# A gated feed-forward kernel with exact weight splits: another maker for the first low chunk, scales three tiles ahead, and a new order in the prologue and the second batch

## The chip, the cores and the metric

One Trainium2 (trn2) chip, one core of it. The metric is the device time of one execution in microseconds (us), as the median of several runs; the profile is of one execution, taken by the hardware profiler. Engines: TensorE (PE), VectorE (DVE), ScalarE (ACT), GpSimd (POOL), and SyncE (SP), whose queue issues nearly all DMAs.

## The reference

x is [8, 512, 512] float32 and cond [8, 128]. With 2048 hidden columns:

```python
scale = cond @ norm_w.T + 1.0
h = x * (scale[:, None, :] * rsqrt(mean(x * x, -1) + 1e-6))
val, gate = split(h @ up_w.T)              # 2 x 2048 columns
h = val * gelu(gate)
h = round_and_clip(h * 127 / max|h|)       # per row, int8 range
w = ternary(down_w)                        # by mean|down_w|
y = h @ w.T (scaled back) + x
```

## The kernel before, in words

The kernel works through eight batches of 512 rows, and within each through 16 stages s, one for each tile of 128 value and 128 gate rows of up_w. TensorE multiplies in float16; each float32 operand is split into a high (its float16 rounding) and a low (the rest), and a product is high x high + high x low + low x high, over two halves of the contraction: six matmuls of 128x256. A stage combines a 2x2 block product from **seven** products p1 to p7 (a Strassen-like scheme, functions p1 to p7, lines 1010 to 1035), of seven weight combinations (A11, S1, S2, S4, A12, S3, A22) and seven of x. So a stage has 42 matmuls.

*Weights.* In batch 0, stage s also makes the weights of tile s+1. SyncE loads the tile into one of three staging buffers wst (load_w, line 327, which waits for the second mix step of the tile three before). VectorE finds a power-of-two scale per row (w_scale, line 723: a reduction over 128x1024 and three tiny operations), in stage s for tile s+2. GpSimd scales and mixes (w_mix, line 450: two scalings, four adds or subtractions; MIX = 6 steps counted by mix_steps) into one of two buffers wf. TensorE transposes the seven blocks in four chunks of 4, 4, 4 and 2 transposes (transpose_w, line 974) into three PSUM banks in turn (WB); chunk 0 waits for all six mix steps. ScalarE rounds each chunk to the high (w_high, line 560), VectorE subtracts to get the low (w_low, line 737), which frees the bank. The slots of tiles 4 to 15 go to a DRAM scratch (store_slot, line 332, 896 KB each) and are read back in each later batch through a ring of four (load_slot, line 336, which waits for p4 of the tile four before).

*Order.* Each engine's program is written out by hand, and each engine takes its instructions in that order. In stage s of batch 0 (lines 1114 to 1140) TensorE does p1, p5, chunk 0 of tile s+1, p4 of stage s-1, p6, chunk 1, p3, a transpose of x of batch 1, p2, chunk 2, p7, chunk 3. ScalarE (lines 646 to 672) takes snapshots of PSUM between the products (snap_u3 of s-1, snap_p1, snap_p5, snap_u2), the two halves of the gelu of s-1, the highs and some work ahead for batch 1 (squares, x_out, x_high in x_ahead, line 612; normalise), and in even stages the sum of absolute values of a piece of down_w (DW_SUM). VectorE (lines 917 to 939) does value(s-1), w_scale(s+2), its passes for x, the lows, hidden(s-1) and, after some stages, the running maximum (largest, over two to four tiles). GpSimd (lines 513 to 521) does gate_second(s-1), w_mix(s+2), then the rsqrt or the x mix. p4 of stage s-1 waits for snap_u3 of s-1.

*SyncE in batch 0* (lines 404 to 410), per s: the load of weight tile s+3, in odd s a piece of down_w (512 KB, once the sum of an earlier one is done), and the store of slot s, which waits for the lows of slot s.

*Prologue.* Scales of x from cond and norm_w, the squares and rsqrt of x, the first weights, the splits of x.

*Batch 1* besides its stages quantises batch 0 (q_scale, q_round, q_clip for one pair of tiles in each of the stages 2 to 9), turns the eight pieces of down_w into ternary form (down_clip on GpSimd at the stages of DW_CLIP, down_round on VectorE at DW_TERN, transpose_dw on TensorE at DW_T), and does the down product of batch 0 in four tiles (down_tile, 16 matmuls of 128x512 each, at the stages of DOWN_AFTER, here 10, 12, 13, 14), whose output VectorE writes a stage later (staged_out). SyncE's order is in its batch, line 359: pieces of down_w (load_dw waits for down_round) stand between slot loads. Batches 2 to 7 are the same without down_w.

## Time and profile before

| | |
|---|---|
| median of 3 runs | 823.17 us (820.63 to 823.93) |
| the profiled execution | 822.39 us, span 820.6 us |
| TensorE busy, mean granted clock | 770.3 us (94%), 0.989 |
| VectorE, ScalarE, GpSimd busy | 616.1, 428.6, 250.9 us |
| DMA | 130.88 MB, 159 GB/s |

The span runs from the first to the last instruction. Busy time counts executing instructions alone. A mean "granted clock" of 1.0 is TensorE at full speed. In the rows, "A <- B" in brackets tells what ended the idle time before an instruction, and L numbers are lines of the kernel.

### The profile page before, as it was taken

How to read it: one execution, taken by the hardware profiler on the slowest of the kernel's cores; microseconds unless marked ns; L12 is line 12 of the kernel's file. 1: busy time of each engine (PE TensorE's matmuls, PEld its weight loads, DVE VectorE, ACT ScalarE, POOL GpSimd, SP SyncE). 2: the span in 40 equal slices, each digit the busy share in tenths (PEclk: the TensorE clock that was granted, in tenths of full speed). 3: DMA queues.
4: the chain of work that ended last, by engine and by line, in shares of the span. 5: the costliest groups of instructions: out<-in, count | busy, mean ns of one | idle time of the engine just before them, and what ended most of it. 6: DMA issues, size and time to landing. Idle time of an engine off the chain costs nothing.

```text
span 820.6 us, 17515 instructions
## 1 busy us (share of the span) xinstructions
PE 770.3 (94%) x6385; PEld 636.2 (78%) x6385; DVE 616.1 (75%) x890; ACT 428.6 (52%) x997; POOL 250.9 (31%) x313
## 2 busy tenths in 40 slices
PE   5788887987999999999999999999999999999987
PEld 4677776875778897789878887789868987888853
DVE  5889798889854896389846895489657994589577
ACT  4677565564544664355543654355535654445523
POOL 4477777343421232112221232123211232111100
PEclk9999999999999999999999999999999999999999
DMA  4546662745455255443456154535545245505512
GB/s 142 208 133 205 192 213 119 295 156 166 177 184 184 65 197 182 136 173 134 149 179 228 53 194 142 187 114 179 170 163 179 94 175 185 186 32 195 187 52 77
DMA packets 34507, 130.88 MB, mean 159 GB/s; under 512 B 3224, under 2 KB 3744, under 8 KB 34464
## 3 DMA queue, kind: packets, MB, share of 16 engines
q1 hardware_dynamic: 34448, 130.30, 47.1%
q8 instruction: 27, 0.44, 0.2%
q14 instruction: 16, 0.13, 0.1%
q10 hardware_dynamic: 16, 0.00, 0.0%
HBM read 110.89 MB, written 19.40 MB: 159 GB/s over the span
## 4 chain that ended last, share of the span: by engine, by line
PE 73%; DVE 5%; DMA 2%; issue 1%; POOL 1%; ACT 1%; SPq 0%; DVEq 0%; POOLq 0%; ACTq 0%
PE A L1003 11%; PE A L1006 11%; PE A L1005 11%; PE Y L1055 11%; PE B L1006 8%; PE B L1003 8%; PE B L1005 8%; DMA xin<-in_x_dram 2%; DVE h L801 1%; PE X L971 1%; DMA dwb<-in_L_cond_down_w_dram 1%; PE X L1043 1%; DVE h L816 0%; DVE mpart L780 0%; DVE wst L848 0%
## 5 line engine op out<-in xcount | busy, mean ns | idle before, releaser
L1003 PE MATMUL A<-xT,wslots 128*128 (+1 forms) x1024 | 282.2, 276 | 14.8 <-ACT snapC L571 8.5
L1005 PE MATMUL A<-xT,wslots 128*128 (+1 forms) x1024 | 282.2, 276 | 0.0
L1006 PE MATMUL A<-xT,wslots 128*128 (+1 forms) x1024 | 282.1, 275 | 0.0
L475 POOL TENSOR_TENSOR snapC<-snapC 128x256 f32<-128x256 f32 x128 | 101.1, 790 | 463.5 <-ACT snapC L571 462.9
L1005 PE MATMUL B<-xT,wslots 128*128 (+1 forms) x768 | 210.2, 274 | 0.0
L1003 PE MATMUL B<-xT,wslots 128*128 (+1 forms) x768 | 210.2, 274 | 0.0
L1006 PE MATMUL B<-xT,wslots 128*128 (+1 forms) x768 | 210.2, 274 | 0.0
L767 DVE SCALAR_TENSOR_TENSOR h<-h,c_all,g 128x512 f32<-128x512 f32 (+1 forms) x128 | 108.3, 846 | 118.7 <-ACT g L594 117.9
L1003 PEld LDWEIGHTS A<-xT,wslots 128*128 128x128 f16 x1024 | 101.2, 99 | 30.9 <-ACT snapC L571 9.8
L1005 PEld LDWEIGHTS A<-xT,wslots 128*128 128x128 f16 x1024 | 101.2, 99 | 15.1
L1006 PEld LDWEIGHTS A<-xT,wslots 128*128 128x128 f16 x1024 | 101.3, 99 | 12.7
L1055 PE MATMUL Y<-dT,q 128*128 128x512 f16 x448 | 101.3, 379 | 2.1 <-DVE wst L826 2.1
L576 ACT ACTIVATE snapPU<-A 128x256 f32<-128x256 f32 x128 | 49.2, 384 | 97.4 <-PE A L1006 97.4
L571 ACT ACTIVATE snapC<-A 128x256 f32<-128x256 f32 x128 | 49.0, 383 | 95.0 <-PE A L1006 94.9
L761 DVE TENSOR_TENSOR h<-B,snapPU 128x512 f32<-128x512 f32 (+1 forms) x128 | 87.4, 683 | 1.2 <-PE B L1006 1.0
L589 ACT ACTIVATE g<-A,c_all 128x256 f32<-128x256 f32 x128 | 60.6, 473 | 46.7 <-PE A L1006 42.8
L1006 PEld LDWEIGHTS B<-xT,wslots 128*128 128x128 f16 x768 | 75.5, 98 | 9.0
L1005 PEld LDWEIGHTS B<-xT,wslots 128*128 128x128 f16 x768 | 75.5, 98 | 8.8
L1003 PEld LDWEIGHTS B<-xT,wslots 128*128 128x128 f16 x768 | 75.5, 98 | 8.4
L1055 PEld LDWEIGHTS Y<-dT,q 128*128 128x128 f16 x448 | 43.8, 98 | 49.1 <-issue 2.3
L780 DVE TENSOR_REDUCE mpart<-h 128x512 f32<-128x1536 f32 (+2 forms) x40 | 81.0, 2025 | 0.2
L801 DVE TENSOR_TENSOR h<-h,S 128x1024 f32<-128x1024 f32 x64 | 77.5, 1211 | 0.7 <-PE S L1049 0.7
(128 smaller groups left out, 920.1 us busy)
## 6 DMA issues: line engine op xcount, KB each, us to landing
wslots<-w_scratch SPq DMA_DIRECT2D x84, 896.0 KB, 4.7
w_scratch<-wslots SPq DMA_DIRECT2D x12, 896.0 KB, 4.6
wst<-in_L_cond_up_w_dram SPq DMA_DIRECT2D x16, 512.0 KB, 6.2
xin<-in_x_dram SPq DMA_DIRECT2D x8, 1024.0 KB, 7.3
dwb<-in_L_cond_down_w_dram SPq DMA_DIRECT2D x16, 512.0 KB, 4.5
wst<-in_x_dram SPq DMA_DIRECT2D x28, 256.0 KB, 5.4
out_dram<-wst SPq DMA_DIRECT2D x28, 256.0 KB, 5.2
xin<-in_x_dram SPq DMA_DIRECT2D x4, 256.0 KB, 5.1
```

The lines of the kernel that those rows point to most:

```text
L475: pool.tensor_tensor(snapC[:, s % 2, 0:H], snapC[:, s % 2, 0:H], snapC[:, s % 2, H:T], ALU.add)\
L571: act.activation(snapC[:, s % 2, 0:H], BA[s % 2][:, 0:H], ACT.Copy).then_inc(u3_snap, 1)
L576: act.activation(snapPU[:, s % 2, 0:H], BA[s % 2][:, 0:H], ACT.Copy).then_inc(p1_snap, 1)
L589: act.activation(g[:, s % 2, 0:H], BA[s % 2][:, 0:H], ACT.Gelu, scale=c_of(b, s, 1))\
L761: dve.tensor_tensor(h_tile(b, s), BB[s % 2][:, :], snapPU[:, s % 2, :], ALU.add).then_inc(val_ready, 1)
L767: dve.scalar_tensor_tensor(out=h_tile(b, s), in0=h_tile(b, s), scalar=c_of(b, s, 0), in1=g[:, s % 2, :], op0=ALU.mult, op1=ALU.mult).then_ ...
L780: dve.tensor_reduce(into[:, :], h_tiles(b, first, n).rearrange("p n t -> p t n"), AX.X, ALU.max, apply_absolute_value=True).then_inc(max_r ...
L801: dve.tensor_tensor(pair, pair, S[:, :].unsqueeze(1).to_broadcast([P, 2, T]), ALU.mult)\
L1003: pe.matmul(into, high, xh, start=(start and kp == 0), stop=False, skip_group_check=not start)
L1005: pe.matmul(into, high, xl, start=False, stop=False, skip_group_check=not start)
L1006: mm = pe.matmul(into, low, xh, start=False, stop=last, skip_group_check=not start)
L1055: mm = pe.matmul(bank[:, :], of[:, s * T + t * P:s * T + (t + 1) * P], dT[:, s, :], start=(s == first), stop=(s == last))
```

## The change

Batch 0: VectorE makes each tile's scale one stage earlier (w_scale(s+3)). TensorE starts chunk 0 after the third mix step. The low of chunk 0 is no longer VectorE's: TensorE adds minus the high to the transposed values in their PSUM bank (subtract_high, one matmul with a negative float16 identity), and ScalarE copies the result out as float16 (w_low_first). VectorE's small products c_first are done in seven instructions instead of 16. The stages of the x passes for batch 1 have tables of their own (..._AT_0), and GpSimd does x mix and rsqrt ahead of w_mix. Prologue: x is loaded ahead of the weights, norm_w through ScalarE's queue; rsqrt ahead of the first mix; two of the four normalising passes go to ScalarE; x is transposed ahead of the weights; highs and lows in another order. Batch 1: pieces of down_w are clipped at stages 0, 1, 2, 4, 5, 7, 8, 9 (rounded one later, transposed two later) instead of 0 to 7, the down tiles come at stages 12 to 15, and slot 15 is loaded ahead of the first output's store. The diff, cut (indentation reduced):

```diff
...
+C_AT = {1: (3, 2), 3: (5, 2), 5: (7, 2), 7: (9, 2), 9: (11, 2), 12: (13, 3)}
...
+SQUARES_AT_0 = {1: (0, 1), 2: (2, 3)}
+RMS_AT_0, REFINE_AT_0, NORMALISE_AT_0 = 3, 4, 4
+XT_AT_0 = {5: 0, 6: 1, 7: 2, 11: 3}
+XF_AT_0 = {5: 0, 6: 1, 10: 2, 11: 3}
+XMIX_AT_0 = {7: 0, 12: 1}
+XHI_AT_0 = {8: 0, 9: 1, 13: 2, 14: 3}
+XLO_AT_0 = {8: 0, 9: 1, 13: 2, 14: 3}
...
-DW_CLIP = {i: i for i in range(PIECES)}
-DW_TERN = {1 + i: i for i in range(PIECES)}
-DW_T = {2 + i: i for i in range(PIECES)}
+DW_CLIP = {s: i for i, s in enumerate((0, 1, 2, 4, 5, 7, 8, 9))}
+DW_TERN = {s + 1: i for s, i in DW_CLIP.items()}
+DW_T = {s + 2: i for s, i in DW_CLIP.items()}
+DOWN_AFTER_1 = {12: 0, 13: 1, 14: 2, 15: 3}
...
+    minus16 = sb("minus16", [P, P], F16)
...
     def store_slot(s):
-        sp.wait_ge(wlo_ready, NC * (s + 1))
+        sp.wait_ge(wlo0_ready, s + 1)
+        sp.wait_ge(wlo_ready, (NC - 1) * (s + 1))
         sp.dma_start(scratch[s - KEPT], wslots[:, slot_of(s), :]).then_inc(w_stored[(s - KEPT) % RING], 16)
...
+        if first:
+            load_slot(b, 15)
         store_y(b - 1, 0)
         load_xres(b - 1, 2)
-        load_slot(b, 15)
+        if not first:
+            load_slot(b, 15)
...
-    sp.dma_start(nw, norm_w.rearrange("(k p) c -> p k c", p=P)).then_inc(norm_w_loaded, 16)
-    load_w(0)
     for t in range(TT):
         sp.dma_start(xin[:, t, :], x_tile(x_v, 0, t)).then_inc(x0_loaded[t], 16)
-    for p in range(1, WSTAGE):
+    for p in range(WSTAGE):
         load_w(p)
...
+    pool.tensor_scalar(minus16[:, :], ident[:, :], -1.0, 1.0, ALU.mult, ALU.mult).then_inc(consts_ready, 1)
     pool.tensor_copy(ident16[:, :], ident[:, :]).then_inc(consts_ready, 1)
...
+    rsqrt(0)
     w_mix(0)
-    rsqrt(0)
     w_mix(1)
     for s in range(FT):
         if s > 0:
             gate_second(0, s - 1)
+        if s == RMS_AT_0:
+            rsqrt(1)
+        if s in XMIX_AT_0:
+            x_mix(1, XMIX_AT_0[s])
         if s + 2 < FT:
             w_mix(s + 2)
-        if s == RMS_AT:
-            rsqrt(1)
-        if s in XMIX_AT:
-            x_mix(1, XMIX_AT[s])
...
+    act.dma_start(nw, norm_w.rearrange("(k p) c -> p k c", p=P)).then_inc(norm_w_loaded, 16)
...
+    def w_low_first(p):
+        blk, n = W_CHUNKS[0]
+        act.wait_ge(wlo_psum, p + 1)
+        act.activation(w_part(p, 1, blk, n), WB[NC * p % 3][:, 0:n * KP * P], ACT.Copy).then_inc(wlo0_ready, 1)
...
     squares(0)
-    for c in range(3):
-        w_high(0, c)
+    act.wait_ge(rstd_ready, 1)
+    for t in range(2, TT):
+        act.activation(xin[:, t, :], xin[:, t, :], ACT.Copy, scale=rstd[:, t:t + 1]).then_inc(xn0_ready, 1)
     act.wait_ge(scl_ready, 1)
     for j in range(KT):
         x_out(0, j, X0[j])
-    for cut in range(2):
-        for kp in range(KP):
-            x_high(0, kp, cut)
+    x_high(0, 0, 0)
+    w_high(0, 0)
+    x_high(0, 1, 0)
+    w_low_first(0)
+    w_high(0, 1)
+    x_high(0, 0, 1)
+    x_high(0, 1, 1)
+    w_high(0, 2)
     w_high(0, 3)
...
         if s + 1 < FT:
             w_high(s + 1, 0)
         if s > 0:
-            act.wait_ge(c_ready, s)
+            act.wait_ge(c_ready, C_OP_OF[s - 1])
             gelu_first(0, s - 1)
         snap_u2(0, s)
         if s + 1 < FT:
+            w_low_first(s + 1)
             w_high(s + 1, 1)
         if s > 0:
             gelu_second(0, s - 1)
         if s + 1 < FT:
             w_high(s + 1, 2)
-        if s == NORMALISE_AT:
+        if s == NORMALISE_AT_0:
             normalise(1)
-        x_ahead(1, s)
+        x_ahead(1, s, SQUARES_AT_0, XF_AT_0, XHI_AT_0)
...
-        for t in range(TT):
+        for t in range(2 if is_first(b) else TT):
...
+    def c_first(p, n):
+        dve.tensor_tensor(c_all[:, VC * p:VC * (p + n)].rearrange("p (n v) -> p n v", v=VC)[:, :, 0:VG],
+                          c_w[:, VG * p:VG * (p + n)].rearrange("p (n v) -> p n v", v=VG),
+                          c_b[:, 0:1].unsqueeze(2).to_broadcast([P, n, VG]), ALU.mult).then_inc(c_ready, 1)
...
-            if not final and s - 1 in DOWN_AFTER:
-                staged_out(b - 1, DOWN_AFTER[s - 1])
+            down_after = DOWN_AFTER_1 if first else DOWN_AFTER
+            if not final and s - 1 in down_after:
+                staged_out(b - 1, down_after[s - 1])
...
-    w_scale(0)
...
+    refine(0)
+    normalise(0)
     dve.wait_ge(bmaxT_psum, 1)
     dve.tensor_reduce(brow[:, :], BA[1][0:B, 0:P], AX.X, ALU.max).then_inc(scl_steps, 1)
-    rms(0)
+    w_scale(0)
...
-    refine(0)
-    normalise(0)
-    w_scale(1)
-    for c in range(3):
-        w_low(0, c)
-    dve.wait_ge(scl_ready, 1)
-    c_first(0)
     for kp in range(KP):
         x_mix_first(kp)
-    for cut in range(2):
-        for kp in range(KP):
-            x_low(0, kp, cut, KP * cut + kp + 1)
+    w_scale(1)
+    x_low(0, 0, 0, 1)
+    x_low(0, 1, 0, 2)
+    w_low(0, 1)
+    x_low(0, 0, 1, 3)
+    x_low(0, 1, 1, 4)
+    w_low(0, 2)
+    w_scale(2)
+    c_first(0, 3)
     w_low(0, 3)
-    w_scale(2)
     for s in range(FT):
         if s > 0:
             value(0, s - 1)
-            if s + 2 < FT:
-                w_scale(s + 2)
-        if s == RMS_AT:
+        if s + 3 < FT:
+            w_scale(s + 3)
+        if s == RMS_AT_0:
             rms(1)
-        if s == REFINE_AT:
+        if s == REFINE_AT_0:
             refine(1)
-        if s in XLO_AT:
-            x_low(1, *divmod(XLO_AT[s], 2), XLO_AT[s] + 1)
+        if s - 1 in XLO_AT_0:
+            x_low(1, *divmod(XLO_AT_0[s - 1], 2), XLO_AT_0[s - 1] + 1)
         if s == FT - 2:
             c_later()
+        if s in C_AT:
+            c_first(*C_AT[s])
         if s + 1 < FT:
-            w_low(s + 1, 0)
-            c_first(s + 1)
             w_low(s + 1, 1)
         if s > 0:
             hidden(0, s - 1)
@@ -940,6 +976,7 @@
...
+    staged_out(0, TT - 1)
...
@@ -964,24 +1001,46 @@
...
-            pe.wait_ge(xn_ready, TT * b + TT)
+            pe.wait_ge(xn_ready, TT * b + 2)
+            if is_first(b):
+                pe.wait_ge(xn0_ready, 2)
...
+    def low_done(at):
+        p, c = divmod(at, NC)
+        if c == 0:
+            pe.wait_ge(wlo0_ready, p + 1)
+        else:
+            pe.wait_ge(wlo_ready, (NC - 1) * p + c)
+    def subtract_high(p):
+        blk, n = W_CHUNKS[0]
+        pe.wait_ge(whi_ready, NC * p + 1)
+        pe.matmul(WB[NC * p % 3][:, 0:n * KP * P], minus16[:, :], w_part(p, 0, blk, n), start=False, stop=True,
+                  skip_group_check=True).then_inc(wlo_psum, 1)
...
         if c == 0:
+            pe.wait_ge(mix_steps, MIX * p + 3)
+        elif c == 1:
             pe.wait_ge(mix_steps, MIX * (p + 1))
         if at >= 3:
-            pe.wait_ge(wlo_ready, at - 2)
+            low_done(at - 3)
         for a in range(n):
             for kp in range(KP):
-                tr = pe.transpose(WB[at % 3][:, (a * KP + kp) * P:(a * KP + kp + 1) * P],
-                                  wf(p)[:, blk + a, kp * P:(kp + 1) * P], ident[:, :])
+                tr = pe.matmul(WB[at % 3][:, (a * KP + kp) * P:(a * KP + kp + 1) * P],
+                               wf(p)[:, blk + a, kp * P:(kp + 1) * P], ident[:, :], is_transpose=True,
+                               start=(a == 0 and kp == 0), stop=(a == n - 1 and kp == KP - 1),
+                               skip_group_check=True)
...
-            pe.wait_ge(wlo_ready, NC * s + CHUNK_OF[a] + 1)
+            low_done(NC * s + CHUNK_OF[a])
...
-            if not final and s in DOWN_AFTER:
-                if first and s == min(DOWN_AFTER):
+            down_after = DOWN_AFTER_1 if first else DOWN_AFTER
+            if not final and s in down_after:
+                if first and down_after[s] == 0:
                     pe.wait_ge(dT_ready, PIECES)
-                down_tile(b - 1, DOWN_AFTER[s])
-
-    pe.wait_ge(consts_ready, 1)
+                down_tile(b - 1, down_after[s])
+    pe.wait_ge(consts_ready, 2)
...
-    for c in range(3):
-        transpose_w(0, c)
     for j in range(KT):
         transpose_x(0, j, X0[j])
+    transpose_w(0, 0)
+    transpose_w(0, 1)
+    subtract_high(0)
+    transpose_w(0, 2)
     transpose_w(0, 3)
...
         p6(0, s)
         if s + 1 < FT:
+            subtract_high(s + 1)
             transpose_w(s + 1, 1)
...
```

## Rows read from the trace of the kernel before

**Rows 1.** The page, busy time, share of the span, instructions.
```profile
PE 770.3 (94%) x6385; PEld 636.2 (78%) x6385; DVE 616.1 (75%) x890; ACT 428.6 (52%) x997; POOL 250.9 (31%) x313
```

**Rows 2.** Windows: busy us of each engine by stretch, clock, DMA.
```profile
core 0: us, PE busy (x) PEld busy (x) DVE busy (x) ACT busy (x) POOL busy (x), PEclk, DMA share, GB/s
...
34.20:148.00 113.80, 96.16 (x813) 83.99 (x811) 95.33 (x171) 76.92 (x178) 80.17 (x102) 0.96 0.51 168
...
152.00:260.00 108.00, 98.04 (x831) 80.11 (x829) 79.85 (x104) 54.21 (x121) 40.36 (x42) 0.97 0.55 191
260.00:350.00 90.00, 89.96 (x762) 74.57 (x760) 66.07 (x91) 46.18 (x112) 20.52 (x26) 1.00 0.47 158
```

**Rows 3.** Timeline, ScalarE: first snapshot of stages 1 and 15 of batch 0.
```profile
35.46 0.39 ACT L576 ACTIVATE snapPU<-A 128x256 f32<-128x256 f32 x1
...
148.16 0.39 ACT L576 ACTIVATE snapPU<-A 128x256 f32<-128x256 f32 x1
```

**Rows 4.** Timeline, TensorE: fourth weight chunk in stages 0 and 1.
```profile
33.86 0.38 PE L983 MATMUL Y<-ident,q 128*128 128x128 f32 x2
...
39.97 0.38 PE L983 MATMUL Y<-ident,q 128*128 128x128 f32 x2
```

**Rows 5.** Waits in 34 to 148 us: us in total, times, longest.
```profile
POOL q L456 <- DVE inv_w L735: 21.8, 13, 4.4
...
PE Y L983 <- POOL q L468: 6.1, 5, 2.1
...
PE S L983 <- POOL q L468: 5.9, 4, 2.4
PE A L1003 <- ACT snapC L571: 5.2, 3, 3.7
...
PE S L983 <- DVE wslots L741: 0.4, 1, 0.4
```

**Rows 6.** Groups by shape in 34 to 148 us: busy us, mean ns.
```profile
L741 DVE TENSOR_TENSOR wslots<-Y,wslots 128x512 f16<-128x512 f32 x28 | 19.1, 683 | 5.2 <-ACT wslots L567 5.0
L567 ACT ACTIVATE wslots<-Y 128x512 f16<-128x512 f32 x28 | 16.8, 599 | 14.0 <-PE Y L983 13.5
...
L462 POOL TENSOR_TENSOR q<-q 128x256 f32<-128x256 f32 x13 | 11.4, 877 | 0.0
...
L468 POOL TENSOR_TENSOR q<-q 128x256 f32<-128x256 f32 x14 | 10.2, 726 | 1.1
...
L669 ACT ACTIVATE dwb<-dwb 128x1024 f32<-128x1024 f32 x8 | 8.4, 1049 | 0.0
```

**Rows 7.** Timeline, stage 12 of batch 0.
```profile
131.52 0.84 ACT L557 ACTIVATE xT<-xf 128x768 f16<-128x768 f32 x1 [4.18 <-POOL xf L483]
...
134.00 0.40 PE L1003 MATMUL A<-xT,wslots 128*128 128x256 f16 x1 [3.66 <-ACT snapC L571]
```

**Rows 8.** Timeline, prologue.
```profile
6.67 0.63 ACT L540 ACTIVATE xf<-xin 128x512 f16<-128x512 f32 x1 [4.00 <-DMA xin<-in_x_dram]
...
12.09 1.03 POOL L448 TENSOR_TENSOR r_pow<-ms,neg_half 128x4 f32<-128x4 f32 x1
...
26.05 0.39 PE L1003 MATMUL A<-xT,wslots 128*128 128x256 f16 x1 [6.27 <-DVE xT L720]
```

**Rows 9.** The tile wst up to 150 us: the landing of its loads.
```profile
DMA to landing us min/median/max: 3.3/6.2/8.8
```

**Rows 10.** Batch 1: waits in 152 to 260 us, SyncE's slot 10, landing.
```profile
PE Y L991 <- DVE wst L848: 6.1, 2, 3.2
...
PE A L1003 <- ACT snapC L571: 3.4, 2, 2.3
...
ACT xT L557 <- POOL xf L483: 1.5, 1, 1.5
...
202.03 0.43 SPq L339 DMA_DIRECT2D wslots<-w_scratch  x1
...
wslots<-w_scratch SPq DMA_DIRECT2D x84, 896.0 KB, 4.7
```

More of the change, by code:

```diff
@@ L61, in gated_ffn_program @@
     B12 = T1
+    C_AT = {1: (3, 2), 3: (5, 2), 5: (7, 2), 7: (9, 2), 9: (11, 2), 12: (13, 3)}
+    C_OPS = 1 + len(C_AT)
+    C_OP_OF = [1 if p < 3 else 1 + next(i + 1 for i, (q, n) in enumerate(C_AT.values()) if p < q + n) for p in range(FT)]
     W_CHUNKS = [(0, 2), (2, 2), (4, 2), (6, 1)]
@@ L262, in gated_ffn_program @@
         rstd_ready = sem("rstd_ready")
+        xn0_ready = sem("xn0_ready")
         xn_ready = sem("xn_ready")
@@ L274, in gated_ffn_program @@
         whi_ready = sem("whi_ready")
+        wlo_psum = sem("wlo_psum")
+        wlo0_ready = sem("wlo0_ready")
         wlo_ready = sem("wlo_ready")
@@ L610, in normalise, with x_ahead @@
                     act.activation(xin[:, t, :], xin[:, t, :], ACT.Copy, scale=rstd[:, t:t + 1]).then_inc(xn_ready, 1)
-            def x_ahead(b, s):
-                if s in SQUARES_AT:
-                    squares(b, SQUARES_AT[s])
-                if s in XF_AT:
-                    x_out(b, XF_AT[s])
-                if s in XHI_AT:
-                    x_high(b, *divmod(XHI_AT[s], 2))
+            def x_ahead(b, s, squares_at=SQUARES_AT, xf_at=XF_AT, xhi_at=XHI_AT):
+                if s in squares_at:
+                    squares(b, squares_at[s])
+                if s in xf_at:
+                    x_out(b, xf_at[s])
+                if s in xhi_at:
+                    x_high(b, *divmod(xhi_at[s], 2))
             def batch(b, first=False, final=False):
@@ L672, in _ @@
                     w_high(s + 1, 3)
-            act.wait_ge(c_ready, FT + VC)
+            act.wait_ge(c_ready, C_OPS + VC)
             batch(1, first=True)
@@ L742, in w_low @@
                     .then_inc(wlo_ready, 1)
-            def c_first(p):
-                pair = slice(VG * p, VG * p + VG)
-                dve.tensor_scalar(c_all[:, VC * p:VC * p + VG], c_w[:, pair], c_b[:, 0:1], None, ALU.mult)\
-                   .then_inc(c_ready, 1)
+            def c_first(p, n):
+                dve.tensor_tensor(c_all[:, VC * p:VC * (p + n)].rearrange("p (n v) -> p n v", v=VC)[:, :, 0:VG],
+                                  c_w[:, VG * p:VG * (p + n)].rearrange("p (n v) -> p n v", v=VG),
+                                  c_b[:, 0:1].unsqueeze(2).to_broadcast([P, n, VG]), ALU.mult).then_inc(c_ready, 1)
             def c_later():
@@ L882, in _ @@
             dve.tensor_copy(cndT, BA[0][:, 0:B]).then_inc(condT_ready, 1)
-            w_scale(0)
+            rms(0)
             dve.wait_ge(scl_psum, 1)
@@ L1130, in _ @@
                 if s + 1 < FT:
+                    subtract_high(s + 1)
                     transpose_w(s + 1, 1)
                 p3(0, s)
-                if s in XT_AT:
-                    transpose_x(1, XT_AT[s])
+                if s in XT_AT_0:
+                    transpose_x(1, XT_AT_0[s])
                 p2(0, s)
```

## The prediction, made before the changed kernel was built or run

> **What bounds the kernel now.** I read the page first: TensorE is busy most of the span and VectorE three quarters of it [rows 1]. Then the windows, by stretch, since these shares are means: batches 2 and later are full, TensorE being busy 89.96 of 90 us there, and nothing in the diff touches their work. What can move is the prologue, batch 0 (113.8 us with TensorE busy 96.2, clock 0.96) and batch 1 (108.0 us with 98.0 busy) [rows 2]. The stage starts give batch 0 its pace: from the second stage's snap at 35.46 to the last one's at 148.16 are 14 stages in 112.7 us, 8.05 us each [rows 3]. The least that TensorE needs is in its fastest stage, from one fourth weight chunk to the next: 39.97 - 33.86 = 6.11 us [rows 4]. So 14 x 6.11 = 85.5, and 4 x 0.44 for the 16 transposes of x that fall into this stretch (0.109 each, as 56 instructions take 6.11): 87.3. The trace shows the stage in full there: 42 products and 14 transposes. **25.4 us are excess.** The chain of waits tells whose: TensorE waits 6.1 + 5.9 = 12.0 us for GpSimd's last mix of a tile, 5.2 for ScalarE's snapshot, 0.4 for a low; GpSimd before it waits 21.8 us in 13 mixes for the scales of VectorE [rows 5]. So the circle is value, scale, mix (two scalings and four adds of 0.73 to 0.88 us, some 4.9 [rows 6]), transpose. The other 7.8 us are hand-offs and the low clock: a mean of 0.96 over 113.8 us is 4.6 us, and the granted clock falls to 1.2 from 2.4 GHz behind long waits; after the wait of 3.66 us a product matmul shows 400 ns where the fastest stage starts an instruction every 0.109 us [rows 4, 7].
>
> **Batch 0, part by part.** *Scales three ahead, mix released after its third step.* The scales of tile s+2 are now written a stage before the mix needs them, so the 21.8 us of GpSimd's wait go. GpSimd's own work is 80.2 us of this stretch, 5.7 per stage [rows 2], and its in-order queue keeps the snapshot sum ahead of the mix, so it still can be late at the two stages with x mixes of some 3.4 us (four adds): I leave 1.0 of the 12.0 us. Gain 11.0.
> *Low of chunk 0 by TensorE and ScalarE.* VectorE loses one pass of 0.683 us per tile, and nine of sixteen tiny products [rows 6]: some 0.8 us of 6.8 per stage (95.3 / 14 [rows 2]). It is not the last releaser in rows 5 except for 0.4 us, so I price the relief at 0.4. TensorE gains one matmul of 512 columns per tile: two 256-column slots of 0.109 us 0.22 x 14 = 3.1 us, all on the path. ScalarE gains a pass of 0.60 us (as its highs of the same shape [rows 6]) per tile: from 76.9 us to 85.3, 6.1 per stage [rows 2], as much as TensorE's 6.3. It stands between the second snapshot and the remaining highs, so highs 1 to 3 and the snapshot that TensorE's fourth product waits for queue behind it. In stages with a down_w sum (1.05 us and its readout [rows 6]), the normalising or an x pass there is no slack. Bounds for what this adds: 0, if it fits into ScalarE's idle time (36.9 us of the stretch, 113.8 - 76.9), and 8.4, if each pass lies on the path; I take 2.5, nearer to nothing since three quarters of those 36.9 us would have to be in the wrong place otherwise.
> *x passes in another order.* At stage 12 ScalarE stood 4.18 us for GpSimd's x mix, and TensorE 3.66 behind it [rows 7]. Mix before w_mix and its high a stage later: that 3.7 goes. rsqrt(1) now stands before a mix, but its input comes some 2 us into the stage, and the mix has a stage of room: nothing, else 1 us.
> *The staging load.* The scale of tile s+3 reads a buffer whose load the SP queue issues only after the store of a slot (896 KB) and in every second stage a down_w piece. These loads land in 3.3 to 8.8 us [rows 9]; by the order of the code the issue is one stage minus 0.2 us ahead of the use where it used to be two. At 7.2 us per stage the slow ones come 1.8 us late, five times; VectorE has about 2.5 us before TensorE feels it, except after the wide maxima. I put 2.0 us on it (0 to 9).
> *Clock and hand-offs.* With the long waits gone, 4.6 us of low clock should shrink to some 1.2: gain 3.4.
> Sum: -11.0 - 0.4 + 3.1 + 2.5 - 3.7 + 2.0 - 3.4 = **-10.9 us**, 7.3 per stage.
> GpSimd's adds take 877 ns on average where the least disturbed ones take 726 [rows 6]. If any VectorE work caused that, less VectorE work would give back about 1 us more over batch 0; I take nothing.
> The Trainium skill (SBUF — State Buffer, section "SBUF: two separate sides") says that the port pair which the two share is an exclusive lock, taken by VectorE only in two-port modes or with two SBUF inputs. By that rule the dropped pass, which reads PSUM, frees nothing, and the sum would stay; no row here separates the two.
>
> **Prologue.** TensorE's first product starts at 26.05. The rsqrt starts at 12.09 though four squares from 6.67 at some 0.67 each are done at 9.4, as GpSimd was in the first mix; the first square waited 4.00 us for its x tile [rows 8]. With x tiles ahead of the weights and rsqrt ahead of the mix, the normalised x is some 4 us earlier. Of that 1.8 us (the scale of tile 0, a pass over 1024 columns and three tiny ones, which VectorE now does before the scales of x that ScalarE's x_out needs) is given back. I take **-2.2 us**; bounds 0 (the second weight scale, 1.8, now ahead of the x lows, is given back too) and -4.
>
> **Batch 1.** Its excess over a full batch is 18 us [rows 2]; the 64 transposes of down_w are in it (at most 7.0, at 0.109) and stay. The 2.3 us wait at stage 3 behind x of the next batch stays, since four slot loads and x are issued as before [rows 10]. Of the 6.1 us in which TensorE waits for the rounding of pieces (stages 6, 7), VectorE's round and one contended pass leave stage 4: -1.3. These two stages still have a round each. The wait of ScalarE for GpSimd at stage 8, 1.5 us, goes, as GpSimd doesn't hang on the last piece's load before it: -1.5. But the SP queue loads piece 7 when the sixth round is done, now at the end of stage 8, and *slot 10 is queued behind it*. Slot loads (896 KB) land in 4.7 us, and with 512 KB ahead in some 6.5 (an estimate: 512/896 of the two thirds of 4.7 that go by size). The round ends some 0.8 us into stage 9, a stage of about 4.6 + 0.4 us, so the slot lands some 2.8 us after TensorE wants it for stage 10, with 0.5 for the issue. Before it went out at 202.03, stages ahead [rows 10]. Bounds 0 (if the round runs early) and 4. Of the down tiles one leaves stage 10 and one enters 15, the same 16 matmuls on TensorE in whichever stage; VectorE's output pass of the last tile falls into the start of batch 2, where ScalarE's gelu ends last: nothing, and one pass of some 0.7 us if that cover is gone. Sum -1.3 - 1.5 + 2.8 = **0**, from -4 to +3.
>
> Total -10.9 - 2.2 + 0 = -13.1. The profiled execution took 822.39 us around its span of 820.6: 809.3. It lies 0.8 below the median of the three runs, so against that, **810 us**. A measurement of this kernel can tell about 0.5% (4.1 us) from no change.
>
> **Rivals.**
> *TensorE becomes the bound.* For it: every other engine has less than 6.3 us of work per stage. Against it: 6.1, 5.9 and 5.7 leave little for in-order queues. Batch 0 is then 87.3 + 3.1 + 1 = 91.4 for 112.7, -21.3; with the prologue -23.5: 799.7. Chance 0.17.
> *The staging load paces batch 0.* The wait for w_loaded takes the place of that for the scales: from VectorE's last low of a stage 8.8 us to the load's landing, then 6.2 us of that later stage, is 15.0 for two stages, 7.5 each, over stages 4 to 12, with the ScalarE terms on top: batch 0 gains some 7, slot 10 costs 4: 815 to 818. Chance 0.14.
> *It doesn't do what it says.* GpSimd, already 5.7 us per stage and without its wait, still delivers mixes as late since the snapshot sum holds it; then only the prologue and stage 12 are left: 819 to 822. Against it: GpSimd's wait in front of the mix is for scales, thirteen times [rows 5]. Chance 0.06.
> *Slower: the ScalarE circle.* High 0, subtract, low 0 are three dependent steps on two in-order queues. If ScalarE's queue ends each stage, already at 8.05 us, 0.60 + 0.22 us add to each: 14 x 0.82 = 11.5, less 2.2: 832. It decides from the point at which ScalarE's idle time ahead of the highs is used up in every stage; 36.9 us of it, 2.6 a stage, speak against it. Chance 0.05.
> *The forecast* itself, with its own range of 803 to 815, has 0.58.
>
> **Numbers.** Faster by over 0.5%: 0.58 + 0.17 + 0.12 of the load case: 0.87. Within 0.5%: 0.02 of that case and the 0.06: 0.08. Slower: 0.05. The range takes in the edge of the TensorE case and the load case: 801 to 819.
>
> **What would show it.** Right: GpSimd's wait for the scales under 3 us; TensorE's on the last mix under 2; stages of batch 0 at 6.9 to 7.6; VectorE waits in front of the scale's reduction on the load; first product at 23.5 to 24.5; a wait of TensorE for a slot load at stage 10 of batch 1, and no change from batch 2 on. Wrong: waits of TensorE on ScalarE over 8 us in batch 0 (ScalarE case), stages at 6.4 (TensorE case), or a batch 1 shorter by over 4 us.

## The result, and the profile after

The changed kernel takes 817.88 us (median of 6 runs, 815.63 to 819.54), the kernel before 822.73 us in the runs beside it: ratio 0.9939, 95% interval 0.992 to 0.9958, so 5 us faster. The profiled execution took 816.54 us around a span of 814.8. I had predicted 810; the time lies in the stated range of 801 to 819, but the gain is less than half of the 13 us I summed.

The page after, span and busy time (answers to [rows 1]):

```profile
span 814.8 us, 17562 instructions
...
PE 771.6 (95%) x6401; PEld 635.3 (78%) x6401; DVE 610.5 (75%) x863; ACT 437.0 (54%) x1015; POOL 251.2 (31%) x314
```

The windows after, for stage 0, the fourteen stages 1 to 14 of batch 0, stage 15, batch 1 and the rest (answers to [rows 2]; columns as there):

```profile
22.87:33.42 10.55, 8.95 (x64) 6.87 (x65) 10.03 (x17) 5.08 (x13) 10.04 (x12) 0.86 0.22 76
33.42:138.81 105.39, 96.18 (x817) 83.92 (x815) 88.33 (x144) 81.64 (x190) 76.85 (x101) 0.97 0.54 182
138.81:143.12 4.31, 4.15 (x39) 3.72 (x39) 3.80 (x5) 2.30 (x8) 0.86 (x2) 1.00 0.74 220
143.12:254.19 111.07, 98.68 (x827) 80.21 (x826) 81.84 (x105) 53.81 (x121) 40.21 (x42) 0.95 0.53 189
254.19:814.00 559.81, 553.05 (x4615) 452.44 (x4613) 413.08 (x560) 280.60 (x666) 114.72 (x141) 1.00 0.44 150
```

The bounds are starts of ScalarE's first snapshot of a stage (the first bound is TensorE's first product). With the same bounds before, [rows 3] gave 112.7 us for stages 1 to 14, and batch 1 had 107.69. So the 5.8 us of span come from three places: **stage 1 begins 2.0 us earlier** (33.42 for 35.46), **stages 1 to 14 take 7.3 us less** (105.4), and **batch 1 takes 3.4 us more** (111.1). From batch 2 on nothing moved.

The length of each stage, as the difference of two such snapshot starts, shows where (us; stage 0 first):

```
batch 0  before   7.9  5.6  9.4  6.1  7.6  7.5  7.3  7.0 12.4  5.8 10.7  7.3 11.6  7.3  7.0  4.3
         after    9.1  6.5  7.4  5.6  9.9  7.8  7.8  7.3  7.6  6.1 10.8  6.1  6.8  8.0  7.6  4.3
batch 1  before   4.6  6.3  7.8  6.3  5.0  5.0  8.5 10.5  6.9  4.8  8.0  5.0  8.0  8.0  8.0  4.7
         after    4.6  6.6  8.3  6.2  5.0  4.6  7.4  8.6  5.0 10.0  7.1  5.5  8.0  8.0  8.0  8.1
```

Stages 8 and 12 of batch 0 lost 4.8 us each. Stage 4 grew by 2.3 and stage 10 stayed at 10.8. In batch 1 stages 6 to 8 lost 4.9 together, while stage 9 more than doubled (in stages 10 and 15 a down tile of some 3.5 us has left and come, so stage 10 is 2.5 us too long).

The waits after, from 20 to 145 us (answers to [rows 5]):

```profile
POOL snapC L496 <- ACT snapC L599: 29.2, 13, 6.8
...
PE S L1040 <- DVE wslots L776: 4.8, 3, 2.1
POOL q L477 <- DVE inv_w L770: 4.2, 1, 4.2
PE A L1062 <- ACT snapC L599: 3.7, 5, 2.1
...
DVE inv_w L761 <- DMA wst<-in_L_cond_up_w_dram: 2.3, 2, 1.9
...
PE Y L1040 <- POOL q L483: 1.3, 2, 1.1
```

GpSimd's 21.8 us of waiting for scales are gone from the stages (the 4.2 left are in the prologue); it now waits for ScalarE's snapshots instead, and TensorE hardly feels that: its 12.0 us of waits for mixes are 1.7, all but 0.2 of them in stage 0. But its wait for a low (L776) went from 0.4 to 4.8 us. Here is that wait at its longest, in the timeline of stages 9 and 10:

```profile
96.43 1.36 DVE L755 TENSOR_TENSOR xT<-xf,xT 128x768 f16<-128x768 f32 x1
97.71 0.69 DVE L780 TENSOR_TENSOR c_all<-c_w,c_b 128x4 f32<-128x4 f32 x1
98.32 0.68 DVE L776 TENSOR_TENSOR wslots<-Y,wslots 128x512 f16<-128x512 f32 x1
98.92 0.81 DVE L802 SCALAR_TENSOR_TENSOR h<-h,c_all,g 128x512 f32<-128x512 f32 x1
99.76 1.92 DVE L815 TENSOR_REDUCE mpart<-h 128x512 f32<-128x1536 f32 x1
...
101.71 1.19 DVE L819 TENSOR_TENSOR m<-m,mpart 128x512 f32<-128x512 f32 x1
...
102.83 0.68 DVE L776 TENSOR_TENSOR wslots<-S,wslots 128x512 f16<-128x512 f32 x1
...
103.65 0.63 PE L1040 MATMUL S<-ident,q 128*128 128x128 f32 x4 [2.11 <-DVE wslots L776]
```

Read it upward: TensorE wants the bank S for the next tile's transposes. The low that frees it is done at 103.5, because VectorE has an x low, a small product and a wide maximum ahead of it. The mean granted clock in 100 to 112 us is 0.86.

Stage 4, ScalarE's and TensorE's timelines:

```profile
58.85 2.54 ACT L638 ACTIVATE xin<-xin,rstd 128x512 f32<-128x512 f32 x4
61.30 1.04 ACT L704 ACTIVATE dwb<-dwb 128x1024 f32<-128x1024 f32 x1
...
62.60 0.37 ACT L599 ACTIVATE snapC<-A 128x256 f32<-128x256 f32 x1
...
63.03 0.28 PE L1062 MATMUL A<-xT,wslots 128*128 128x256 f16 x1 [2.09 <-ACT snapC L599]
```

The normalising came from stage 5 to stage 4, an even stage with a sum over down_w, and the snapshot that TensorE's product p4 needs is behind both.

Batch 1: SyncE's queue and TensorE at stage 10:

```profile
200.39 0.33 SPq L366 DMA_DIRECT2D dwb<-in_L_cond_down_w_dram  x1
...
200.76 11.47 SPq L358 DMA_DIRECT2D wslots<-w_scratch  x4
...
207.86 0.40 PE L1062 MATMUL A<-xT,wslots 128*128 128x256 f16 x1 [4.14 <-DMA wslots<-w_scratch]
```

Slot 10 goes out at 200.76 behind the last piece of down_w and is there, by the end of TensorE's wait, 7.1 us later (207.86 - 200.76). TensorE stands 4.14 us, and the window of the next 8.6 us shows a clock of 0.67, where half speed (1.2 GHz for 2.4) would be 0.5:

```profile
207.86:216.48 8.62, 8.62 (x58) 6.84 (x59) 4.83 (x6) 3.90 (x9) 1.24 (x2) 0.67 0.61 235
```

The prologue, in the timeline (answers to [rows 8]):

```profile
7.76 1.03 POOL L469 TENSOR_TENSOR r_pow<-ms,neg_half 128x4 f32<-128x4 f32 x1 [5.64 <-DVE ms L724]
...
22.87 0.40 PE L1062 MATMUL A<-xT,wslots 128*128 128x256 f16 x1 [2.32 <-DVE xT L755]
```

rsqrt starts 4.3 us and the first product 3.2 us earlier. Stage 0 is then 1.1 us longer: TensorE waits 1.12 and 0.45 us in it for GpSimd's mix, in a stretch of 10.55 us in which VectorE is busy 10.03 and GpSimd 10.04.

The 2.0 us gained at the start of stage 1 are those of one profile. Six other profiles below have the same prologue and stage 0 (e1, e2, e5, e6, e11, e12), and there stage 1 begins at 33.42 to 35.27, between 0.2 and 2.0 us ahead of the old 35.46. Much of what differs is the clock: product matmuls start every 0.213 us at first and every 0.109 us later, and the faster rhythm is there by 27.2 us in this profile, in e1 only from 31.8.

### The profile page after: what moved, and what is told of

It is laid out like the page before. It is cut to its first block, busy times and chain, and to the rows that moved or that the text cites. A ratio compares the mean times of both kernels' runs of the same rounds, so it can differ in the third digit from the quotient of the medians.

```text
span 814.8 us, 17562 instructions
## 1 busy us (share of the span) xinstructions
PE 771.6 (95%) x6401; PEld 635.3 (78%) x6401; DVE 610.5 (75%) x863; ACT 437.0 (54%) x1015; POOL 251.2 (31%) x314
## 4 chain that ended last, share of the span: by engine, by line
PE 72%; DVE 6%; DMA 3%; issue 1%; ACT 1%; SPq 0%; DVEq 0%; ACTq 0%
PE A L1062 11%; PE A L1065 11%; PE A L1064 11%; PE Y L1114 11%; PE B L1065 8%; PE B L1062 8%; PE B L1064 8%; DVE h L836 2%; DMA xin<-in_x_dram 2%; PE X L1010 1%; DMA wslots<-w_scratch 1%; DMA w_scratch<-wslots 1%; DVE h L802 1%; PE X L1102 1%; DVE h L851 0%
## 5 line engine op out<-in xcount | busy, mean ns | idle before, releaser
L802 DVE SCALAR_TENSOR_TENSOR h<-h,c_all,g 128x512 f32<-128x512 f32 (+1 forms) x128 | 106.6, 833 | 122.8 <-ACT g L622 122.1
```

What stands on the lines that cost most here:

```text
L802: dve.scalar_tensor_tensor(out=h_tile(b, s), in0=h_tile(b, s), scalar=c_of(b, s, 0), in1=g[:, s % 2, :], op0=ALU.mult, op1=ALU.mult).then_ ...
```

## The experiments

Ratios are to the kernel before in the same session, with the 95% interval. The changed kernel's is 0.9939 (0.992 to 0.9958). One interval is some 2 us to either side (3 for e5), so single edits that differ by less are told apart by their traces or not at all. A difference of a few us between the stage lengths of two profiles can also be one of TensorE's clock, and the text names it where it matters.

| run | edit to the changed kernel | median us | ratio (interval) |
|---|---|---|---|
| e1 | slot 10 ahead of the last piece | 815.36 | 0.9902 (0.9877, 0.9927) |
| e2 | batch 1 as before | 814.79 | 0.9907 (0.9882, 0.9932) |
| e3 | low of chunk 0 on VectorE | 817.66 | 0.9935 (0.9913, 0.9957) |
| e4 | scales two ahead | 817.98 | 0.9935 (0.9911, 0.9959) |
| e9 | scales two ahead, mix released at six | 829.52 | 1.0092 (1.0061, 1.0124) |
| e10 | x passes as before | 816.63 | 0.9923 (0.9901, 0.9946) |
| e5 | sum of stage 4 to stage 3 | 813.75 | 0.9892 (0.9854, 0.9931) |
| e6 | maximum after the lows | 817.82 | 0.9939 (0.9915, 0.9963) |
| e11 | e2 + e5 | 811.33 | 0.9854 (0.9831, 0.9877) |
| e12 | e11 + stage 9 relieved | 810.05 | 0.984 (0.9819, 0.9862) |
| e13 | e2 + e10 | 814.01 | 0.9887 (0.9867, 0.9907) |
| e14 | *kernel before*, mix released at three | 817.64 | 0.9931 (0.991, 0.9953) |

### Batch 1: the queue behind the last piece

e1:
```diff
                 load_slot(b, 9)
                 if first:
+                    load_slot(b, 10)
                     load_dw(7, PIECES + 7)
-                for s in range(10, 15):
+                for s in range(11 if first else 10, 15):
```


> The changed kernel with one edit in SyncE's order: slot 10 is loaded ahead of the last piece of down_w. Theory A (slot 10, queued behind that piece, is what batch 1 lost): TensorE's 4.1 us wait for a slot load at stage 10 and the half-speed matmuls behind it go, batch 1 gets 5 to 6.5 us shorter than the changed kernel's 111.1, total 811 to 813. Theory B (the link is saturated whichever transfer goes first): slot 10 or 11 is late all the same, or the last piece is late for its clip and the down tiles, and the total stays at 816 to 819.

e2:
```diff
-    DW_CLIP = {s: i for i, s in enumerate((0, 1, 2, 4, 5, 7, 8, 9))}
-    DOWN_AFTER_1 = {12: 0, 13: 1, 14: 2, 15: 3}
+    DW_CLIP = {i: i for i in range(PIECES)}
+    DOWN_AFTER_1 = DOWN_AFTER
```
(and SyncE's load of slot 15 and the last staged_out where they were)

> The changed kernel with batch 1 as before (pieces of down_w at stages 0 to 7, down tiles at 10, 12, 13, 14, SyncE's old order). Theory A: the new batch 1 costs 3.4 us net by the traces (111.1 against 107.7), so undoing it alone gives 813.5 to 815.5, and the waits at stages 6 to 8 (8 us) come back while the one for slot 10 goes. Theory B (batch 1 is only shifted by where batch 0 ends, and would be as long in either order): no change, 816.5 to 819.

e1 gave 815.36, 2.5 us better than the changed kernel and between the ranges of my two theories. The wait for the slot is gone from TensorE's list and stage 9 is 6.6 us for 10.0, but stage 10 is still 6.7, and batch 1 109.5 us long. The trace names what is late next, the rounding of the pieces, now three times:

```profile
PE Y L1051 <- DVE wst L884: 6.5, 3, 2.9
```

e2, in theory A's range, gave 814.79 with batch 1 at 108.4 us: stages 6 to 8 are long again (8.1, 10.6, 6.9 us), and 9 and 10 are as before (4.8, and 8.0 with its down tile). So the slot load was the largest loss of the new batch 1, but its gain at stages 6 to 8, 4.9 us, was also partly a move: with fewer roundings there, the ones moved to stages 9 and 10 stand in front of TensorE too.

### Batch 0: the scale and mix chain

e4:
```diff
-                if s + 3 < FT:
-                    w_scale(s + 3)
+                if s > 0 and s + 2 < FT:
+                    w_scale(s + 2)
```
(and each entry of C_AT a stage later where the scale is)

> The changed kernel with scales two tiles ahead again. Theory A (the scales were the wait that paced batch 0): GpSimd's wait for them comes back with some 20 us in all, TensorE's for the mixes with over 5, batch 0 gets 5 to 8 us longer, 823 to 826. Theory B (GpSimd's wait was only slack, and the other edits carried the gain): within 1.5 us of the changed kernel's 817.9, with TensorE's wait for mixes under 3 us since the mix is released after its third step.

e9, e4 and:
```diff
                 if c == 0:
-                    pe.wait_ge(mix_steps, MIX * p + 3)
-                elif c == 1:
                     pe.wait_ge(mix_steps, MIX * (p + 1))
```


> The changed kernel with scales two tiles ahead and the mix released after all six steps: the whole scale-mix chain as before. Theory A (the two edits stand in for each other; either of them breaks the old circle): now GpSimd's mix comes late again, TensorE waits for it with 4 to 8 us, total 822 to 825. Theory B (the chain was late only where the x passes, the order of GpSimd and the chunk-0 low made it late): within 1.5 us of the run that has the scales back alone, 817 to 819.

e14, in the kernel before:
```diff
                 if c == 0:
+                    pe.wait_ge(mix_steps, MIX * p + 3)
+                elif c == 1:
                     pe.wait_ge(mix_steps, MIX * (p + 1))
```


> The kernel before with one edit: chunk 0 waits for the third mix step instead of the sixth (chunk 1 for the sixth). Theory A (that wait alone broke the old circle, the scales three ahead being its stand-in): TensorE's 12 us of waits for mixes fall under 5, batch 0 5 to 8 us shorter, total 815 to 818. Theory B (in the old frame, with the chunk-0 low on VectorE and x passes in between, an earlier chunk 0 only moves the wait to chunk 1 or to a low): 820 to 823, and TensorE's waits for lows or ScalarE grow by what the mixes lose.

e4 was the surprise: **theory B**. GpSimd waits 13.5 us for scales again, and the time is the same (817.98), with stages 1 to 14 at 104.7 us. In e4's waits TensorE has 3.2 us on mix steps, not 12, the two largest groups of it here:

```profile
POOL q L477 <- DVE inv_w L770: 13.5, 9, 2.1
...
PE Y L1040 <- POOL q L483: 1.7, 3, 1.1
PE Y L1040 <- POOL q L489: 0.9, 1, 0.9
```

With the earlier release undone as well the time is 829.5 us, 11.6 above the changed kernel and 6.5 above the kernel before (822.99 in that session), beyond the 822 to 825 of theory A. GpSimd's wait is back at its old size and TensorE waits for the last mix step (L489):

```profile
POOL q L477 <- DVE inv_w L770: 19.9, 10, 4.2
...
PE Y L1038 <- POOL q L489: 11.0, 7, 3.3
...
PE S L1038 <- POOL q L489: 3.4, 2, 2.4
```

So the early release breaks the circle, and the scales three ahead add nothing to it. Whether the scales alone, with the release after six steps, would have broken it too, no run shows. e9 also tells what the rest of the change does without the release: against the kernel before, stage 1 begins 1.9 us later, stages 1 to 14 take 1.1 us more (113.8) and batch 1 3.6 more (111.3).

I had not let the change's early release into the sum as an edit of its own at all. And e14 asks the other way round: the old kernel with the early release alone, a change to one wait, takes 817.64 us, ratio 0.9931: **as much as the whole change gave**. Stages 1 to 14 take 108.0 us for 112.7, about half of this by a mean granted clock of 0.97 for 0.95; batch 0 and all before it are 5.6 us shorter at the start of batch 1 (146.90 for 152.48). Its waits show that the scales are nearly as late as ever, and that TensorE no longer minds:

```profile
POOL q L456 <- DVE inv_w L735: 19.0, 12, 4.4
...
PE A L1005 <- ACT snapC L571: 10.2, 5, 4.7
...
PE S L985 <- DVE wslots L741: 2.8, 3, 1.4
PE Y L985 <- DVE wslots L741: 1.3, 1, 1.3
```

What it minds is ScalarE's snapshot (10.2 us for 5.2 in [rows 5]), with stages 8 and 12, the x mixes, still at 12.3 and 11.6 us. And it waits 4.1 us for lows, for 0.4 before, though nothing in VectorE's program was changed.

### Batch 0: the low of chunk 0

e3:
```diff
-                    w_low_first(s + 1)
...
-                    subtract_high(s + 1)
...
                 if s + 1 < FT:
+                    w_low(s + 1, 0)
                     w_low(s + 1, 1)
```
(likewise in the prologue, with the old counts of wlo_ready)

> The changed kernel with the low of chunk 0 back on VectorE (no subtract on TensorE, no extra ScalarE pass); batch 0 then has scales three ahead and the new x passes alone. Theory A (ScalarE's extra pass and TensorE's subtract cost about what VectorE's relief gives): within 2 us of the changed kernel, 816 to 820. Theory B (VectorE is what ends the stages now): 5 to 8 us slower, 823 to 826. Theory C (ScalarE is, and its late snapshots): 3 to 5 us faster, 813 to 815.

817.66 us: **theory A**, the extra pass and the extra matmul cost what they give. But not because nothing happens. TensorE's window of the 14 stages is 106.2 us long, VectorE is busy 95.6 of them (88.3 in the changed kernel), and TensorE's waits for lows more than double:

```profile
PE Y L1036 <- DVE wslots L773: 6.3, 6, 1.5
PE S L1036 <- DVE wslots L773: 5.5, 3, 2.7
```

With the low on VectorE, VectorE is thus what TensorE waits for most: 11.8 us for 4.8. The change's move of the low relieves TensorE of 7 us of such waiting. No run separates what takes this back, but the traces name two parts. The 14 subtract matmuls are 3.1 us; three of them stand directly in front of a wait of TensorE (1.03, 2.11 and 1.69 us) and fill time that was idle, so some 2.4 us count. The other part is the clock, whose mean in these stages is 1.00 in e3 and 0.97 in the changed kernel (some 3.2 us):

```profile
34.96:141.20 106.24, 91.15 (x808) 80.40 (x806) 95.64 (x159) 76.68 (x175) 73.99 (x101) 1.00 0.54 180
```

e10 and e11 below have 1.00 there too, with the low as in the change. So the slow stretches are no price of the subtract, and the move may be worth some 3 us that this pair of profiles hides; the medians (817.66 and 817.88) don't show it. The first product also comes later with the low on VectorE (ScalarE's first snapshot at 26.30 for 24.37).

### Batch 0: the x passes, stage 4 and stage 10

e10:
```diff
-    SQUARES_AT_0 = {1: (0, 1), 2: (2, 3)}
-    RMS_AT_0, REFINE_AT_0, NORMALISE_AT_0 = 3, 4, 4
+    SQUARES_AT_0 = SQUARES_AT
+    RMS_AT_0, REFINE_AT_0, NORMALISE_AT_0 = 4, 5, 5
```
(the other tables alike; on GpSimd rsqrt and x mix behind w_mix)

> The changed kernel with the x passes of batch 0 at their old stages and GpSimd's rsqrt and x mix behind the weight mix. Theory A (the order of the x passes carries most of the gain of batch 0: stages 8 and 12 fell from 12.4 and 11.6 us to 7.6 and 6.8): stages 8 and 12 over 10 us again, stage 4 back from 9.9 to under 8, batch 0 5 to 7 us longer, total 822 to 825. Theory B (scales and mixes carry it): stage 12 alone comes back, 3 us or less, 819 to 821.

e5:
```diff
-    DW_SUM = {2 * i: i for i in range(PIECES)}
+    DW_SUM = {(3 if i == 2 else 2 * i): i for i in range(PIECES)}
```


> The changed kernel with one ScalarE pass moved: the sum of the third down_w piece from stage 4, where the normalising now is, to the empty stage 3. Theory A (stage 4's 9.9 us come from ScalarE's queue, with 2.5 + 1.25 us of extra passes ahead of the last high and the snapshot): TensorE's 2.1 us wait for that snapshot falls below 1 and the half-speed stretch behind it goes; stage 4 at 8 to 8.7, total 815 to 816.5. Theory B (the stage is held by the low of VectorE or by the load): under 0.7 us of change, 817.5 to 818.5.

e10 fell outside both theories: 816.63 us, if anything a little below the changed kernel. Stages 8 and 12 go to 9.4 us (for 7.6 and 6.8), not over 10, and stages 4, 13 and 14 give 3.7, 1.9 and 1.2 back (6.2, 6.1 and 6.4 for 9.9, 8.0 and 7.6); stages 1 to 14 take 102.9. The new order of the x passes cured two stages and broke three others. That the sum is 2.5 us shorter with the old order isn't shown to come from it: the mean granted clock of these stages is 1.00 in e10 for 0.97, which alone is worth more.

e5 shows what the coincidence with the sum costs: one pass and its accumulation (1.04 + 0.19 us) moved to an empty stage give 813.75 us, better than my 815. That is 4.1 us by the medians, with an interval that overlaps the changed kernel's; in the profiles, stages 1 to 14 are 2.2 us shorter (103.2). TensorE's wait there goes from 2.1 to 1.5 only, stage 4 from 9.9 to 8.8, and stage 5 from 7.8 to 6.1, since it no longer starts at half speed. I had expected the wait to fall below 1 (missed) and the slow stretch to go (it did): most of the gain is clock.

e6:
```diff
                     hidden(0, s - 1)
-                    largest(0, s - 1)
                 if s + 1 < FT:
                     w_low(s + 1, 2)
                     w_low(s + 1, 3)
+                if s > 0:
+                    largest(0, s - 1)
```


> The changed kernel with the running maximum of VectorE behind the third and fourth low of each stage in batch 0 instead of ahead of them. Theory A (stage 10's 10.8 us, and TensorE's 4.8 us of waits for lows, are the wide maximum and an x low ahead of a low that frees a bank): the waits for lows fall below 1.5 us, stage 10 to under 8.5, total 813 to 815.5. Theory B (VectorE has too much work whatever its order: the wait moves to the next value or low): total within 1 us of the changed kernel, with waits of ScalarE or TensorE on VectorE elsewhere.

**Theory B.** 817.82 us, nothing. The longest stall moved from stage 10 (9.9 us, with a wait of 1.89 left) to stage 8 (12.1 us), where the maximum over four tiles, with its second pass of 1.08 us, now stands on VectorE from 78.50 to 83.4. The value pass of the next stage comes behind it, then the scale and a small product, and the low is done at 87.4 only:

```profile
87.59 0.73 PE L1041 MATMUL S<-ident,q 128*128 128x128 f32 x4 [2.63 <-DVE wslots L776]
```

e11 and e12 put the pieces together; e12 has in addition:
```diff
-                if s - 1 in XLO_AT_0:
+                if s - 1 in XLO_AT_0 and s != 9:
...
                     w_low(s + 1, 3)
+                if s == 9:
+                    x_low(1, 0, 0, 1)
```
(and C_AT's entry at stage 9 at stage 10)

> The changed kernel with batch 1 as before and the down_w sum of stage 4 at stage 3. Theory A (the two losses are apart: 3.1 us of batch 1 and 4.1 us of stages 4 and 5): they add, 810 to 812. Theory B (part of what stage 4 gave came back in batch 1 because it began at another moment): 812.5 to 814.

> As the run before, and in stage 9 the x low (0.95 us) is behind the lows and the small product of two columns' worth (0.7 us) a stage later, so 1.6 us less of VectorE's work stand ahead of the third low of stage 9, which TensorE waited 2.1 us for at stage 10. Theory A (that queue is stage 10's 10.8 us): the wait falls under 0.7 us, no half-speed stretch follows, stage 10 at 7 to 8.5, total 2 to 4 us below the run before. Theory B (VectorE is merely late by a fixed amount): the stall moves to a later stage, as when the maximum was moved, total within 1 us of the run before.

e11: 811.33 us, 1.5% below the kernel before: the two repairs add. Its interval lies clear of the changed kernel's and of e14's, so once the two losses are repaired the rest of the change is worth something beyond the early release; which part of it, no run says. e12: 810.05, not told apart from e11. The wait at stage 10's second chunk (2.11 us in the changed kernel) is gone, but the x lows still stand ahead of a low there, and the wait comes back some 3.6 us later in the trace, as 1.42 us. Stage 10 is 9.6 us, for 10.8 in the changed kernel and 10.1 in e11:

```profile
104.87 1.55 DVE L752 TENSOR_TENSOR xT<-xf,xT 128x1024 f16<-128x1024 f32 x1
...
107.24 0.63 PE L1038 MATMUL S<-ident,q 128*128 128x128 f32 x4 [1.42 <-DVE wslots L773]
```

e13 has the edits of e2 and e10.

> The changed kernel with both batch 1 and the x passes as before; what is left of the change are scales, mix release, chunk-0 low and the prologue. Theory A (the new x order costs 1 to 2 us, the new batch 1 some 3, independent of each other): 812.5 to 814.5. Theory B (with the old x passes ending later, batch 1 of the old kind suffers): 815 to 817.

814.01 us, as theory A has it, but its profile shows batch 0 short (102.9) and batch 1 long: 111.2 us in an order that took 107.7 to 108.4 in five other profiles (before, e2, e11, e12, e14). The window shows what is longer:

```profile
142.11:253.35 111.24, 100.74 (x827) 81.48 (x826) 78.11 (x104) 54.06 (x120) 39.48 (x42) 0.94 0.54 185
```

TensorE's mean granted clock is 0.94 there for 0.97 in the other five, which is some 3.3 us of 111; its waits are no longer than in e2 (10.5 us in all, for 10.6). Whether the batch got this clock from how it was entered or by chance, one profile can't say.

## Why the prediction was right and wrong

**Right.** The bound and its circle; the disappearance of GpSimd's wait for the scales and of TensorE's for the mixes (12.0 us to 0.2 in stages 1 to 14, I had 1.0 left, 11.0 gained); no change from batch 2 on; the place and the mechanism of the slot load at stage 10 of batch 1; the gains at stages 6 to 8, -4.9 for my -2.8 (2.3 to 5.1 in the seven other profiles with this order), with 1.4 us less waiting for the rounding of pieces for my 1.3.

**Right in part by luck, the prologue:** -2.0 for -2.2. The first product came at 22.87, ahead of my 23.5 to 24.5, and stage 0, which I had not priced, gave 1.1 us of it back. In the six other profiles with the same prologue the gain is 0.2 to 2.0 us.

**Wrong, batch 0: -7.3 for -10.9.** The failing step is "It is not the last releaser in rows 5 except for 0.4 us, so I price the relief at 0.4". I read VectorE's slack off a trace in which another engine was late, and let it stand for the new one. TensorE's waiting for lows was to go from 0.4 us to nothing and went to 4.8, a miss of 4.8 us, larger than the whole miss of batch 0. e14, in which VectorE's work is untouched, shows that the rhythm does it: there the early release alone takes these waits from 0.4 to 4.1 us. e3 shows that the relief was worth more than 0.4 in waiting: without it the waits are 11.8 us. VectorE's own work (88.3 of 105.4 us) comes in lumps, maxima, x lows and products ahead of a low that frees a bank. The remaining terms: subtract 2.4 for my 3.1, since 3 of the 14 matmuls fall into waits; snapshots 3.7 us now where I had 5.2 - 3.7 + 2.5 = 4.0; low clock 0.97 of 105.4 us is 3.2 for my 1.2, with slow stretches behind the stalls of stages 4 and 10; the staging load made VectorE wait 2.3 us in two waits, and no wait of TensorE is put down to it, so my 2.0 there looks too much. With the mixes, 0.8 us better than I had them, the terms add up to a miss of 3.0 us, for 3.6 measured.

**Wrong, the attribution.** I credited the scales three ahead and the early release together with 11.0 us and the x passes with 3.7. The runs: the scales three ahead, nothing on top of the release (e4), and never run without it; release alone, 5 us and more even in the old kernel (e14); both gone, +11.6 (e9); x passes, nothing that shows (e10): what stages 8 and 12 gained was paid with stages 4, 13 and 14. Stage 4's collision was to be seen in the tables: the normalising at 4, the sums at every even stage. I wrote that there was "no slack" in such stages and priced all of them at 2.5 us; that one stage and the slow stretch behind it cost 2.2 us by e5's profile and 4.1 by its median.

**Wrong, batch 1: +3.4 for 0.** The failing step is the term "so the slot lands some 2.8 us after TensorE wants it". The wait was 4.14 us (the slot landed in 7.1 us, not 6.5, and the round ended about when I had it). That two thirds of a landing go by size, on which my 6.5 rested, no row showed. And I put no price on the clock behind it, although [rows 7] had shown one: stage 10 is 2.5 us too long beside, and the mean granted clock of the batch went from 0.97 to 0.95, some 2 of its 3.4 us. My bounds for the batch, -4 to +3, just missed.

**The rivals.** TensorE as the bound: not reached, stages 7.5 us on average. The staging load pacing batch 0: refuted, 2.3 us of waits. The ScalarE circle: refuted, snapshot waits fell from 5.2 to 3.7 us. "It doesn't do what it says": GpSimd's waiting shifted to the snapshots exactly as described, but its mixes were in time all the same.

## What to carry to other kernels

When a wait between two engines is removed, an engine whose idle time you count as slack has that slack only in the old rhythm: ask which of its instructions frees what the fast engine needs next, and what lumps stand in front of it. Before building the large reordering, try the smallest edit of the wait itself: here a semaphore count that asks for three steps instead of six gave as much as the whole change. When two edits aim at the same wait, run each of them alone. And when work is moved between hand-written tables, add up each engine's extras stage by stage, and for a DMA queue what is next behind each waiting issue; both losses here were readable that way.

## What the runs showed of the hardware that I had not expected

A stall of TensorE can cost more than its length, and the same stall doesn't always. After the wait of 4.14 us the 8.6 us that followed ran at a mean granted clock of 0.67, which at two levels of 1.2 and 2.4 GHz is about two thirds of them at half speed, some 2.8 us lost; after the 2.11 us at stage 10 of batch 0 the window of 12 us has 0.86, 1.7 us lost. But e11 has the same wait of 2.11 us at the same place, and its clock from 100 to 112 us is 1.00; e3 has one of 2.74 us (at 82.3) and 1.00 in the 12 us behind it. So part of the differences between two profiles here, up to some 3 us in stages 1 to 14 and as much in batch 1, is whether the clock fell behind a stall that both have.

The granted clock in the first microseconds has to be read with care. e11's window from 23 to 27 us gives 1.00, while its product matmuls start every 0.213 us there and every 0.109 later. I therefore compare clocks only behind stage 0.

GpSimd's instructions can take up to three times their time beside VectorE. In stage 0 after, two scalings that take 0.69 us elsewhere took this, while VectorE ran x lows with both inputs in SBUF:

```profile
21.19 2.10 POOL L477 TENSOR_SCALAR q<-wst,inv_w 128x512 f32<-128x512 f32 x1 [4.16 <-DVE inv_w L770]
...
23.27 1.76 POOL L479 TENSOR_SCALAR q<-wst,inv_w 128x512 f32<-128x512 f32 x1
```

The rule of the Trainium skill (SBUF — State Buffer, section "SBUF: two separate sides") is an exclusive lock on the ports that the two engines share, which a VectorE operation with two SBUF inputs takes for its whole length. The trace agrees here. With the low that reads PSUM back on VectorE (e3), GpSimd was busy 74.0 us in the 14 stages, not more than the 76.9 of the changed kernel, so that pass does not hold GpSimd up, as the rule has it.
